# Routed layers of a decoder kernel: gated slot results scattered into pairs of rows, read back by plain loads, with 23 and 31 steps

## The chip, the cores and the metric

The kernel runs on one core of one Trainium2 chip. The metric is the device time of one execution in microseconds (us); lower is better. TensorE, VectorE (DVE in the rows), ScalarE (ACT), GpSimd (POOL) and SyncE (SP) each run their own list of instructions in order and wait for each other on semaphores. DMA transfers are issued from SP's and POOL's queues.

## The reference

A residual stream x of 4 x 512 tokens (T = 2048) and 512 features goes through four attention-like layers and four feed-forward layers. The change is in the last and the third feed-forward layer, which are routed:

```python
# ffn2: 8 experts, inner size 352, top 2, gates renormalised
topk_w, topk_i = jax.lax.top_k(softmax(x @ gate_w.T), 2)
topk_w = topk_w / jnp.sum(topk_w, axis=-1, keepdims=True)
for e in range(8):
    w_e = jnp.sum(jnp.where(topk_i == e, topk_w, 0.0), axis=-1)
    out = out + w_e[:, None] * ((silu(x @ w_gate[e]) * (x @ w_up[e])) @ w_down[e])
# ffn3: 16 routed experts, inner size 256, gelu, top 2, gates not renormalised,
# and two shared experts for all tokens
x = x + tanh(g_ffn[i]) * out          # x inside the layer is its layer norm
```

## The kernel before

Each token takes two experts, so there are 4096 pairs of token and choice. `router_block` computes the logits, takes the top two, counts the tokens per expert and gives each pair a slot; each expert's slots begin at a multiple of 256. A step is 256 slots of one expert. The number of steps, NS, is fixed: 2T/256 + experts = 24 in ffn2 and 32 in ffn3. By matmuls with one-hot matrices (hot_p, hot_h) the router inverts the map: `step_token` says for each slot which token it holds. `step_expert` holds each step's expert, `slot` each pair's slot, and `gates` its weight, times tanh of the layer's gate.

`routed_block` then runs the loop over steps. Two buffers, w = 0 and 1, alternate. In the order of their names in the code:

- SP: load(s+2) brings the expert's weights to mo_up (up32) and mo_dn (dn32), once step s's are split into halves; store(s-1) waits for the results of s-1 (o_done) and writes mo_o (o32) to `slot_results`.
- POOL: gather(s+1) waits until step s-1 was transposed (g_T), copies two columns of step_token (L810), and fetches 2 x 128 rows of the normalised x by indirect DMA (L814) into mo_g.
- TensorE: transposes of s+1 (L852), the up matmuls of s (L867), the down matmuls of s-1 (L882). TensorE's step s therefore starts with the transposes of s+1.
- ScalarE: y_high(s+1) (L904), per chunk the silu or gelu (L926, L928) and the high half of mid (L932), with the high halves of the next weights between (L911, L918); results(s-1) (L938) moves the down result from PSUM to mo_o.
- VectorE: the low half of each of these (L962, L967, L974, L984) and in ffn2 the product (L981).

All precise values are kept as a high and a low half in f16, with three matmuls in place of one.

After the loop comes the read-back: POOL waits for all stores, and gathers for each token tile of 128 the two result rows (L835), four indirect DMAs for two tiles. VectorE multiplies by the gates (L1011, L1016), adds to x (L1019) and computes bn_stats (L1023) for the next layer norm. At the end of the program `store_block` writes x with one DMA of 4 MB (L3357). Blocks follow one another; all engines meet between them. The names in rows leave out a block's number, so mo_ stands for both layers.

Of the kernel before, what the change touches and what calls it, by code (L numbers as in the profile page):

```python
# [16 lines left out]
P = 128  # L17
# [236 lines left out]
SLOTS = 256  # L254
ROUND = 12582912.0


def router_block(nc, env, y_hi, y_lo, w_router, n_exp, coef, routing, th, down_scale, renorm, shared):
# [7 lines left out]
    gates, slot, step_expert, step_token = routing  # L266
    NS = step_expert.shape[1]
    with ExitStack() as ctx:
# [13 lines left out]
        slotf, tile = sb("slotf", [P, NT, 2]), sb("tile", [P, NT, 2])  # L282
        stepi, stepf, owner = sb("stepi", [P, NS], I32), sb("stepf", [P, NS]), sb("owner", [P, NS])
# [3 lines left out]
        hot_h = sb("hot_h", [P, NT * 2, 2 * NS], F16)  # L287
        p_rank, p_total = ps("rank", [P, NT, n_exp]), ps("total", [P, NT, n_exp])
        p_token = ps("slot_token", [P, 2 * NS])
        tri_clear, tri_done, hot_ready, counted = sem("tri_clear"), sem("tri"), sem("one_hots"), sem("counted")  # L290
        placed, inverted = sem("places"), sem("inverted")
# [14 lines left out]
        def _(pool):  # L306
# [3 lines left out]
            nc.gpsimd.iota(ramp_p[:], pattern=[[1, P]], base=0, channel_multiplier=0).then_inc(ramp_done, 1)  # L310
            nc.gpsimd.memset(ones[:], 1.0).then_inc(tri_done, 1)
# [14 lines left out]
        def _(pe):  # L326
# [16 lines left out]
            for n in range(2 * NT):  # L343
                last = nc.tensor.matmul(p_token[:], hot_p[:, n, :], hot_h[:, n, :], start=(n == 0), stop=(n == 2 * NT - 1))
            last.then_inc(inverted, 1)

        @block.vector
        def _(dve):
# [4 lines left out]
            dve.wait_ge(ramp_done, 4)  # L353
# [26 lines left out]
            c.link(nc.vector.tensor_scalar(gates[:], tops[:], cs[:], None, ALU.mult))  # L380
# [5 lines left out]
            c.link(nc.vector.tensor_copy(stepf[:], stepi[:]))  # L386
            dve.wait_ge(counted, 2)
# [17 lines left out]
            c.link(nc.vector.tensor_copy(slot[:], slotf[:]))  # L405

            for i in (tokenf, token), (ramp_pf, ramp_p):
                c.link(nc.vector.tensor_copy(i[0][:], i[1][:]))
# [6 lines left out]
            def spread(v, n):  # L415
# [5 lines left out]
            h4 = hot_h[:].rearrange("p (t j) h -> p t (j h)", j=2)  # L421
            nc.vector.tensor_tensor(h4, h4, tokenf[:].unsqueeze(2).to_broadcast([P, NT, 4 * NS]), ALU.mult
                                    ).then_inc(placed, 1)
# [8 lines left out]
            c.link(nc.vector.tensor_copy(step_token[:], p_token[:]))  # L432
# [266 lines left out]
def routed_block(nc, env, rows, slots_out, w_up, w_down, kind, inner, routing):  # L699
# [4 lines left out]
    gates, slot, step_expert, step_token = routing  # L704
# [10 lines left out]
    CT = HS  # L715
    with ExitStack() as ctx:
# [11 lines left out]
        cur_slot = sb("cur_slot", [P, 2, CT, 2], I32)  # L728

        back = [t[:].rearrange("p w h d -> p (w h) d").rearrange("p (j u) d -> p j u d", j=2) for t in (g, o32)]  # L730
# [5 lines left out]
        g_in, back_in = ([env.dma_sem(f"{n}{i}") for i in range(2)] for n in ("rows_in", "results_in"))  # L736
# [4 lines left out]
        dn_done, o_done, stored, all_stored = sem("down_done"), sem("out_done"), [sem("out0"), sem("out1")], sem("stored")  # L741
        slot_done, added = sem("slot_cur"), sem("x_added")
        add_own, load_go = sem("add_dve"), sem("load_go")
        block = ctx.enter_context(nc.Block())

        def run_steps(engine, step):

            for s in range(2):
                step(s, s, s < 1, s < 2, False)
            with engine.Fori(1, NS // 2 - 1) as i:  # L750
                step(i * 2, 0, False, False, False)
                step(i * 2 + 1, 1, False, False, False)
            for s in (NS - 2, NS - 1):
                step(s, s % 2, False, False, s == NS - 1)
# [9 lines left out]
        def _(sp):  # L764
# [24 lines left out]
            def store(s, w):  # L789
                sp.wait_ge(o_done, HS * (s + 1))  # L790
                sp.sem_inc(load_go, 1)
                sp.dma_start(slots_out[bass.ds(s * SLOTS, SLOTS), :].rearrange("(h p) d -> p h d", p=P),
                             o32[:, w, :, :]).then_inc(stored[w], 16)
            for w in range(2):
                sp.sem_inc(stored[w], 16)
# [3 lines left out]
            store(NS - 1, 1)  # L799
            sp.wait_ge(stored[0], 16 * (NS // 2 + 1))  # L800
            sp.wait_ge(stored[1], 16 * (NS // 2 + 1))
            sp.sem_inc(all_stored, 1)

        @block.gpsimd
        def _(pool):
# [2631 lines left out]
```

## Time and profile before

| | |
|---|---|
| median of 3 runs | 3375.85 us (3372.21 to 3376.14) |
| the profiled execution | 3385.13 us, its span 3383.4 us |
| mean granted TensorE clock | 0.879 |
| busy over the span | TensorE 74%, VectorE 66%, ScalarE 47%, GpSimd 33% |
| ffn2: loop, read-back | 1851.5 to 2181.2, then to 2244.9 us |
| ffn3: loop, read-back, store | 3089.7 to 3306.7, to 3368.6, to 3383.4 us |

The profiled execution is a run of its own, so its time is not among the three. A duration in a row is that of one instruction or group; "idle before" with an arrow names what ended the wait. Records of DMA instructions on a queue are the issue alone; the landing is given apart. The other layers, from 0 to 1767 us and from 2246 to 2922 us, are the same in both kernels.

### The profile page before, as it was taken

The numbers are of one execution on the slowest core, as the hardware profiler recorded it, in microseconds if no ns is written. First come the engines' busy times: TensorE is split into PE (matmuls) and PEld (weight loads), VectorE is DVE, ScalarE is ACT, GpSimd is POOL, SyncE is SP. The second block draws the span as 40 slices with busy tenths as digits, with TensorE's granted clock in tenths as the row PEclk, the third lists the DMA queues.
The fourth block names the chain that finished last, engine by engine and source line by source line (L and its number), as shares of the span: only waits on it lengthen the run. The fifth ranks groups of instructions, "written<-read, shape, count | busy, mean of one in ns | idle before, by whom it ended". The sixth has DMA issues, their size and how long they took to land. (4 is left out here: it accounts for less than half of the span.)

```text
span 3383.4 us, 41979 instructions
## 1 busy us (share of the span) xinstructions
PE 2518.9 (74%) x14172; PEld 1210.4 (36%) x14172; DVE 2237.8 (66%) x3608; ACT 1606.1 (47%) x2265; POOL 1125.3 (33%) x814
## 2 busy tenths in 40 slices
PE   2987997799788727666653999719788888668990
PEld 1532333344343202222222777505322222334660
DVE  6665763444366788998986666565688884646664
ACT  2544554254334645545532555415476674224870
POOL 5755764010001126666651222155500000002434
PEclk9988999899889858899985999959799999778995
DMA  3640221110000000000003777536402201104995
GB/s 128 203 166 22 80 78 75 59 63 1 4 1 12 0 1 0 0 0 0 0 0 117 233 248 234 157 106 218 168 8 76 63 14 63 51 25 155 316 304 167
DMA packets 162836, 306.01 MB, mean 90 GB/s; under 512 B 33300, under 2 KB 80672, under 8 KB 160247
## 3 DMA queue, kind: packets, MB, share of 16 engines
q1 hardware_dynamic: 139462, 223.49, 19.1%
q0 software_dynamic: 23216, 80.49, 8.3%
q8 instruction: 90, 1.47, 0.2%
q14 instruction: 68, 0.55, 0.1%
HBM read 210.34 MB, written 93.32 MB: 90 GB/s over the span
## 5 line engine op out<-in xcount | busy, mean ns | idle before, releaser
L2054 DVE TENSOR_REDUCE ac_nmax<-ac_M 128x1 f32<-128x512 f32 (+1 forms) x768 | 497.2, 687 | 152.2 <-PE ac_M L1868 147.6
L2032 ACT ACTIVATE ac_PT<-ac_S 128x1024 f32<-128x1024 f32 x384 | 371.2, 1017 | 161.1 <-PE ac_S L1903 142.9
L3190 POOL TENSOR_TENSOR sc_hc<-sc_h,sc_cs 128x1024 f32<-128x1024 f32 x128 | 300.6, 2354 | 172.1 <-DVE sc_h L3304 119.6
L3304 DVE TENSOR_TENSOR_SCAN sc_h<-sc_dA,sc_dB 128x1024 f32<-128x1024 f32 x128 | 292.1, 2283 | 7.0 <-ACT sc_dA L3270 7.0
L3225 PE MATMUL sc_y<-sc_hc,ident 128*128 128x512 f32 x512 | 253.8, 626 | 2.6 <-POOL sc_hc L3190 2.6
L3270 ACT ACTIVATE sc_dA<-ss_delta,sc_A 128x511 f32<-128x511 f32 x256 | 166.0, 682 | 31.7 <-DVE sc_h L3304 31.4
L3203 PE MATMUL sc_b<-ss_bc,sc_sel 128*128 128x512 f16 x128 | 54.7, 428 | 162.0 <-DVE sc_dB L3296 128.7
L3296 DVE TENSOR_TENSOR sc_dB<-ss_du,sc_b 128x1024 f32<-128x1024 f32 x128 | 156.1, 1220 | 27.9 <-PE sc_b L3203 16.9
L3275 ACT ACTIVATE sc_cs<-sc_c 128x512 f32<-128x512 f32 x128 | 76.2, 596 | 202.6 <-POOL sc_hc L3190 159.5
L1868 PE MATMUL ac_M<-KT,QT 64*128 64x512 f16 (+1 forms) x384 | 141.6, 431 | 40.3 <-DVE ac_nmax L2054 23.2
L814 POOL DMA_INDIRECT mo_g<-normalised,mo_cur x112 | 145.3, 1297 | 61.3 <-POOL mo_cur L810 44.2
L967 DVE SCALAR_TENSOR_TENSOR mo_up16l<-mo_up,mo_up16h 128x1408 f16<-128x1408 f32 (+1 forms) x80 | 117.1, 1465 | 71.2 <-ACT mo_up16h L911 70.8
L810 POOL COPY mo_cur<-step_token 128x2 int32 (+1 forms) x56 | 15.4, 276 | 394.4 <-PE mo_yT L852 265.1
L867 PE MATMUL mo_pu<-mo_y16h,mo_up16h 128*128 128x256 f16 (+1 forms) x832 | 127.5, 276 | 25.7 <-DVE mo_up16l L967 11.0
L3225 PEld LDWEIGHTS sc_y<-sc_hc,ident 128*128 128x128 f32 x512 | 104.2, 204 | 99.1 <-issue 80.0
L1868 PE MATMUL ac_M<-ac_KT,ac_QT 64*128 64x512 f16 (+1 forms) x384 | 122.3, 386 | 23.2 <-DVE ac_nmax L2054 18.2
L1922 PE MATMUL ac_o<-ac_PT,ac_V 128*32 128x512 f32 x1024 | 137.9, 611 | 0.2
L1383 PE MATMUL ap_t<-ident,ap_y 128*128 128x128 f32 x128 | 20.4, 284 | 148.6 <-DVE ap_y L1569 148.6
L974 DVE SCALAR_TENSOR_TENSOR mo_dn16l<-mo_dn,mo_dn16h 128x1024 f16<-128x1024 f32 x80 | 83.0, 1062 | 71.5 <-ACT mo_dn16h L918 67.3
L867 PE MATMUL mo_pu<-mo_y16l,mo_up16h 128*128 128x256 f16 (+1 forms) x832 | 126.3, 275 | 0.0
L867 PE MATMUL mo_pu<-mo_y16h,mo_up16l 128*128 128x256 f16 (+1 forms) x832 | 126.0, 274 | 0.0
L932 ACT ACTIVATE mo_mid16h<-mo_mid 128x256 f16<-128x256 f32 x136 | 56.6, 417 | 132.3 <-DVE mo_mid L981 125.3
(515 smaller groups left out, 6102.3 us busy)
## 6 DMA issues: line engine op xcount, KB each, us to landing
slot_results<-mo_o SPq DMA_DIRECT2D x56, 512.0 KB, 3.9
mo_up<-in_w_gate SPq DMA_DIRECT2D x24, 704.0 KB, 5.5
mo_up<-in_w_up SPq DMA_DIRECT2D x24, 704.0 KB, 7.0
keys_t<-ap_kto SPq DMA_DIRECT2D x32, 512.0 KB, 2.6
queries_t<-ap_qto SPq DMA_DIRECT2D x32, 512.0 KB, 2.6
mo_up<-in_exp_up SPq DMA_DIRECT2D x32, 512.0 KB
mo_dn<-in_exp_down SPq DMA_DIRECT2D x32, 512.0 KB
mo_dn<-in_w_down SPq DMA_DIRECT2D x24, 512.0 KB
```

The costliest lines, as they stand in the source:

```text
L814: pool.indirect_dma_start(g[:, w, h, :], None, rows, bass.IndirectOffsetOnAxis(cur[:, w, h:h + 1], 0)).then_inc(g_in[w], 16)
L867: last = nc.tensor.matmul(pu[q][0:n, j, :], up16[h][:, w, j, k, c * P:c * P + n], y16[a][:, w, k, :], start=(i == 0), stop=(i == len(passe ...
L967: nc.vector.scalar_tensor_tensor(out=up16[1][:, w, j, :, :], in0=up32[:, w, j, :, :], scalar=SW, in1=up16[0][:, w, j, :, :], op0=ALU.mult, ...
L1868: nc.tensor.matmul(psM[:, slot, :], QT[b % 2][base:base + n, c, j * P:(j + 1) * P], KT[b % 2][base:base + n, :, c, :], start=True, stop=Tr ...
L1922: last = nc.tensor.matmul(po[r * VC:(r + 1) * VC, :], V[b % 2][:, kt, g % NG * GH + r, :], PT[:, m % PTB, i, :], start=(kt == 0), stop=(kt ...
L2032: nc.scalar.activation(PT[:, n % PTB, :, :], psS[:, 2 * (n % 2):2 * (n % 2) + 2, :], ACT.Exp, scale=SCALE / (SQK * SQK)).then_inc(exp_done, 1)
L2054: last = v.tensor_reduce(out[:, :, 0], sc[:, 0:MAIN], AX.X, ALU.max)
L3190: nc.gpsimd.tensor_tensor(hc[:, m % RC, :, :], h[:, m % RH, :, :], cs[:, m % 2, :].unsqueeze(1).to_broadcast([P, W, S]), ALU.mult).then_in ...
L3225: last = nc.tensor.matmul(py[:, c, :], env.id32[:], hc[:, m % RC, c, :], start=(n == 0), stop=(n == NS - 1))
L3270: last = nc.scalar.activation(dA[:, m % 2, c, 1:S], delta[:, b * KD + k, 1:S], ACT.Exp, scale=A[:, k, n:n + 1])
L3296: nc.vector.tensor_tensor(dB[:, m % RB, :, :], chans(du, b, p), pb[:].unsqueeze(1).to_broadcast([P, W, S]), ALU.mult).then_inc(dB_done, 1)
L3304: nc.vector.tensor_tensor_scan(h[:, m % RH, :, :].rearrange("p c s -> p (c s)"), dA[:, m % 2, :, :].rearrange("p c s -> p (c s)"), dB[:, m ...
```

## The change

1. The router also computes, for each slot, the row in a new tensor `result_pairs` (two rows per token, one per choice; slots without a token get a row of their own behind) and the slot's gate. For that it inverts two more one-hot products: the choice, and the gate in a high and a low half. `gates` and `slot` are gone.
2. ScalarE scales the results by the gate as it moves them to mo_o. It first copies the step's two gate columns.
3. POOL scatters mo_o by indirect DMA into `result_pairs` where SP stored it to `slot_results`. The gathers are issued one place earlier in POOL's order: gather(s+2), then the scatter of s-1.
4. The read-back is a plain SP load of 512 KB per token tile into four buffers of their own. VectorE adds the two rows, adds them to x, and computes bn_stats in ffn2 only. In ffn3 SP stores each tile of x as soon as it is done; `store_block` is gone.
5. NS is (2T + 255 x experts) / 256, rounded down: 23 and 31. The loop is unrolled for the first four steps.

```diff
@@ router_block
-            c.link(nc.vector.tensor_scalar(gates[:], tops[:], cs[:], None, ALU.mult))
+            c.link(nc.vector.tensor_copy(top_h[:], tops[:]))
+            c.link(nc.vector.tensor_tensor(rest[:], tops[:], top_h[:], ALU.subtract))
+            c.link(nc.vector.tensor_scalar(top_l[:], rest[:], GATE_LOW, None, ALU.mult))
+            c.link(nc.vector.tensor_copy(trashf[:], trash[:].rearrange("p s h -> p (s h)")))
...
-            c.link(nc.vector.tensor_copy(slot[:], slotf[:]))
...
+            for i, part in enumerate((top_h, top_l)):
+                last = nc.vector.tensor_tensor(hot_g[:, :, i, :], hot_h[:], spread(part[:], 2 * NS), ALU.mult)
+            last.then_inc(gates_placed, 1)
...
-            c.link(nc.vector.tensor_copy(step_token[:], p_token[:]))
+            c.link(nc.vector.tensor_scalar(step_token[:], p_token[:, 0, :], -1.0, 0.0, ALU.add, ALU.max))
+            c.link(nc.vector.scalar_tensor_tensor(out=pad[:], in0=p_token[:, 0, :], scalar=0.0, in1=trashf[:],
+                                                  op0=ALU.is_equal, op1=ALU.mult))
+            c.link(nc.vector.tensor_scalar(rowf[:], p_token[:, 0, :], 2.0, -2.0, ALU.mult, ALU.add))
+            c.link(nc.vector.tensor_tensor(rowf[:], rowf[:], p_token[:, 1, :], ALU.add))
+            c.link(nc.vector.tensor_tensor(step_row[:], rowf[:], pad[:], ALU.add))
+            dve.wait_ge(gates_inverted, 1)
+            c.link(nc.vector.tensor_scalar(pad[:], p_gate[:, 1, :], 1.0 / GATE_LOW, None, ALU.mult))
+            c.link(nc.vector.tensor_tensor(pad[:], pad[:], p_gate[:, 0, :], ALU.add))
+            c.link(nc.vector.tensor_scalar(step_gate[:], pad[:], cs[:], None, ALU.mult))
@@ routed_block, SP
-                if not first:
-                    store(s - 1, 1 - w)
...
+            for w in range(2):
+                sp.wait_ge(placed_rows[w], 16 * HS * ((NS + 1 - w) // 2))
+            def fetch(t):
+                sp.dma_start(back[:, t % NBK, :, :], pairs[2 * t * P:2 * (t + 1) * P, :].rearrange("(p j) d -> p j d", j=2)
+                             ).then_inc(back_in[t % NBK], 16)
+            for t in range(NBK):
+                fetch(t)
+            for t in range(NT):
+                sp.wait_ge(x_done, t + 1)
+                if t + NBK < NT:
+                    fetch(t + NBK)
+                if final:
+                    sp.dma_start(env.out[t * P:(t + 1) * P, :], env.x[:, t, :]).then_inc(x_out, 16)
@@ routed_block, POOL
+            def place_rows(s, w):
+                if not (isinstance(s, int) and s < 2):
+                    pool.wait_ge(placed_rows[w], 8 * HS * (turns(s, w) - 2))
+                    pool.sem_inc(g_go, 1)
+                nc.gpsimd.tensor_copy(cur_row[:, w, :], step_row[:, bass.ds(s * HS, HS)]).then_inc(row_done, 1)
+                pool.wait_ge(row_done, s + 1)
+                pool.sem_inc(g_go, 1)
+                pool.wait_ge(o_done, HS * (s + 1))
+                pool.sem_inc(g_go, 1)
+                for h in range(HS):
+                    pool.indirect_dma_start(pairs, bass.IndirectOffsetOnAxis(cur_row[:, w, h:h + 1], 0), o32[:, w, h, :], None).then_inc(placed_rows[w], 16)
+
             def step(s, w, first, early, last):
-                if not last:
-                    gather(s + 1, 1 - w, not first)
+                if not (isinstance(s, int) and s + 2 >= NS):
+                    gather(s + 2, w, True)
+                if not first:
+                    place_rows(s - 1, 1 - w)
@@ routed_block, ScalarE
+                nc.scalar.activation(cur_gate[:, w, :], step_gate[:, bass.ds(s * HS, HS)], ACT.Copy).then_inc(gate_done, 1)
+                act.wait_ge(gate_done, s + 1)
+                act.sem_inc(act_go, 1)
                 for h in range(HS):
                     act.wait_ge(dn_done, HS * s + h + 1)
-                    nc.scalar.activation(o32[:, w, h, :], po[h][:], ACT.Copy).then_inc(o_done, 1)
+                    nc.scalar.activation(o32[:, w, h, :], po[h][:], ACT.Copy, scale=cur_gate[:, w, h:h + 1]).then_inc(o_done, 1)
@@ routed_block, VectorE
+            for t in range(NT):
+                dve.wait_ge(back_in[t % NBK], 16 * (t // NBK + 1))
+                a, b = back[:, t % NBK, 0, :], back[:, t % NBK, 1, :]
+                nc.vector.tensor_tensor(a, a, b, ALU.add).then_inc(pair_done, 1)
+                dve.wait_ge(pair_done, t + 1)
+                nc.vector.tensor_tensor(env.x[:, t, :], env.x[:, t, :], a, ALU.add).then_inc(x_done, 1)
+                if not final:
+                    dve.wait_ge(x_done, t + 1)
+                    nc.vector.bn_stats(out=env.stats[:, t, :], in_=env.x[:, t, :])
@@ layer_ffn
-        NS = 2 * T // SLOTS + n_exp
+        NS = (2 * T + n_exp * (SLOTS - 1)) // SLOTS
```

In the rows of order below, the name in brackets is the semaphore waited for, under the name of its first use in the program. This is POOL's queue in the loop of ffn3, one step of it, before; row_in1_79 is g_T:

```order
L808 ISA
L810 ISA [waits row_in1_79]
L810 COPY mo_cur<-step_token 128x2
L811 ISA
L814 DMA mo_g<-normalised,mo_cur 128x512 [waits out_read_138]
L814 DMA mo_g<-normalised,mo_cur 128x512
```

And the same step now, where mid_hi_134 is g_T, q_roots_50 the landed scatters of the same buffer, and vd_out1_68 is o_done:

```order
L839 ISA [waits mid_hi_134]
L839 COPY mo_cur<-step_token 128x2
L840 ISA
L843 DMA mo_g<-normalised,mo_cur 128x512 [waits down_done_136]
L843 DMA mo_g<-normalised,mo_cur 128x512
L848 ISA
L850 ISA [waits q_roots_50]
L850 COPY mo_cur_row<-step_row 128x2
L851 ISA
L853 ISA [waits vd_out1_68]
L856 DMA result_pairs<-mo_o,mo_cur_row 12032x512 [waits first_batch_in_69]
L856 DMA result_pairs<-mo_o,mo_cur_row 12032x512
```

Behind each pair of gathers there now stand a copy, a wait for the step's results, and two scatters; the next gather comes after them.

On ScalarE, at the results in ffn3's loop, before (v_out1_66 is the down matmuls' semaphore, q_out0_63 the landed store):

```order
L935 ISA
L937 ISA [waits q_out0_63]
L938 ACTIVATE mo_o<-mo_po 128x512 [waits v_out1_66]
L937 ISA
L938 ACTIVATE mo_o<-mo_po 128x512 [waits v_out1_66]
```

and now (k_final_51 is the landed scatters, vd_out0_67 the end of the gate copy, ac_dve_70 the down matmuls):

```order
L962 ISA
L964 ISA [waits k_final_51]
L964 ACTIVATE mo_cur_gate<-step_gate 128x2
L965 REGISTER_ALU
L968 ISA [waits vd_out0_67]
L969 ACTIVATE mo_o<-mo_po,mo_cur_gate 128x512 [waits ac_dve_70]
L968 ISA
L969 ACTIVATE mo_o<-mo_po,mo_cur_gate 128x512 [waits ac_dve_70]
```

A copy of 128x2 and a wait for its own end stand ahead of the two activations.

At the end of the program on SP, before (v_out0_65 is o_done):

```order
L792 DMA slot_results<-mo_o 128x2x512 [waits v_out0_65] x3
L716 UNCONDITIONAL_BRANCH [waits q_out1_64,q_out0_63]
L3355 UNCONDITIONAL_BRANCH [waits barrier_Pool_Activation_PE_DVE_SP_release]
L3357 DMA out_x<-x_res 128x16x512
L3351 UNCONDITIONAL_BRANCH [waits k_T_57]
```

and now (k_out0_61 is x_done):

```order
L820 DMA mo_back<-result_pairs 128x1024 [waits k_final_51,q_roots_50]
L820 DMA mo_back<-result_pairs 128x1024 x3
L820 DMA mo_back<-result_pairs 128x1024 [waits k_out0_61]
L829 DMA out_x<-x_res 128x512
L820 DMA mo_back<-result_pairs 128x1024 [waits k_out0_61]
L829 DMA out_x<-x_res 128x512
```

SP issues the loads of the pairs itself, and a tile's store follows the addition to that tile.

## Rows read from the trace of the kernel before

**Rows 1.** Windows: start:end, length, busy us of each engine, clock, DMA share, GB/s.
```profile
1600.00:1700.00 100.00, 64.98 (x167) 25.56 (x166) 92.28 (x56) 54.45 (x85) 63.89 (x28) 0.95 0.00 0
...
1864.00:2168.00 304.00, 290.85 (x2237) 225.87 (x2236) 192.85 (x251) 180.83 (x297) 61.89 (x60) 1.00 0.72 229
...
2181.20:2244.90 63.70, 0.00 (x0) 0.00 (x0) 37.08 (x64) 0.00 (x0) 39.10 (x40) 0.53 0.49 140
...
3089.70:3306.70 217.00, 201.97 (x1408) 142.79 (x1408) 136.15 (x160) 169.88 (x288) 83.77 (x90) 0.98 0.90 297
```
**Rows 2.** The chain that ended last, ffn3's loop: start us, us, what.
```profile
3083.66 6.01 DMA mo_g<-normalised,mo_cur
...
3089.72 1.98 PE mo_yT L852 x8
...
3107.20 0.87 PE mo_yT L852 x8
...
3291.11 0.87 PE mo_yT L852 x8
...
3306.09 0.61 ACT mo_o L938
```
**Rows 3.** Timeline of ffn3's loop: start us, us, engine, what, idle before.
```profile
3113.12 1.04 PE L852 MATMUL mo_yT<-ident,mo_g 128*128 128x128 f32 x8
...
3119.20 1.04 PE L852 MATMUL mo_yT<-ident,mo_g 128*128 128x128 f32 x8
...
3119.40 0.60 ACT L938 ACTIVATE mo_o<-mo_po 128x512 f32<-128x512 f32 x1 [0.39 <-PE mo_po L882]
...
3120.25 0.40 SPq L792 DMA_DIRECT2D slot_results<-mo_o  x1
...
3120.51 0.18 POOL L810 COPY mo_cur<-step_token 128x2 int32 x1 [2.09 <-PE mo_yT L852]
...
3121.48 1.56 POOL L814 DMA_INDIRECT mo_g<-normalised,mo_cur  x1 [0.79 <-POOL mo_cur L810]
...
3123.35 1.16 POOL L814 DMA_INDIRECT mo_g<-normalised,mo_cur  x1 [0.31 <-issue]
```
**Rows 4.** ffn3's gathers: by group (busy, mean ns), by tile (ns least/median/most).
```profile
L814 POOL DMA_INDIRECT mo_g<-normalised,mo_cur x56 | 70.4, 1258 | 30.6 <-POOL mo_cur L810 22.0 <-issue 8.6
...
L814 POOL DMA_INDIRECT mo_g<-normalised,mo_cur x56: 960/1158/1968, 3102.6 to 3281.0; - x56
```
**Rows 5.** mo_g in ffn2's loop, from the start of the instruction.
```profile
DMA to landing us min/median/max: 4.3/4.4/5.4
```
**Rows 6.** Timeline of ffn2's loop.
```profile
2031.94 1.06 ACT L938 ACTIVATE mo_o<-mo_po 128x512 f32<-128x512 f32 x2
...
2037.32 0.64 PE L867 MATMUL mo_pu<-mo_y16h,mo_up16h 128*96 128x256 f16 x4 [0.54 <-DVE mo_mid L981]
...
2043.87 1.04 PE L852 MATMUL mo_yT<-ident,mo_g 128*128 128x128 f32 x8
...
2045.30 1.06 ACT L938 ACTIVATE mo_o<-mo_po 128x512 f32<-128x512 f32 x2
```
**Rows 7.** ScalarE's groups by form, the smallest activation.
```profile
L145 ACT ACTIVATE tanh_gates<-su_graw 128x8 f32<-128x8 f32 x1 | 0.2, 208 | 8.1 <-DMA su_graw<-in_g_ffn 8.1
```
**Rows 8.** Timeline of VectorE in ffn2's router.
```profile
1837.33 1.76 DVE L422 TENSOR_TENSOR rt_hot_h<-rt_hot_h,rt_tokenf 128x1536 f16<-128x1536 f16 x1
...
1841.81 0.21 DVE L432 CAST step_token<-rt_slot_token 128x48 int32<-128x48 f32 x1
```
**Rows 9.** Groups in ffn2's read-back.
```profile
L1023 DVE BATCH_NORM_STATS2 x_stats<-x_res x16 | 10.2, 681 | 0.0
...
L1019 DVE TENSOR_TENSOR x_res<-x_res,mo_g 128x512 f32 x8 | 5.1, 685 | 0.0
```
**Rows 10.** DMA issues: count, KB each, median us from issue to landing.
```profile
f_up<-in_up_weight_t SPq DMA_DIRECT2D x8, 512.0 KB, 4.3
...
out_x<-x_res SPq DMA_DIRECT2D x1, 4096.0 KB, 12.6
```

More of the change, by code:

```diff
@@ L343, in _ @@
             for n in range(2 * NT):
-                last = nc.tensor.matmul(p_token[:], hot_p[:, n, :], hot_h[:, n, :], start=(n == 0), stop=(n == 2 * NT - 1))
+                nc.tensor.matmul(p_token[:, 0, :], hot_p[:, n, :], hot_t[:, n, :], start=(n == 0), stop=(n == 2 * NT - 1))
+            for n in range(1, 2 * NT, 2):
+                last = nc.tensor.matmul(p_token[:, 1, :], hot_p[:, n, :], hot_h[:, n, :], start=(n == 1),
+                                        stop=(n == 2 * NT - 1))
             last.then_inc(inverted, 1)
+            pe.wait_ge(gates_placed, 1)
+            for n in range(2 * NT):
+                last = nc.tensor.matmul(p_gate[:], hot_p[:, n, :], hot_g[:, n, :, :], start=(n == 0),
+                                        stop=(n == 2 * NT - 1))
+            last.then_inc(gates_inverted, 1)
         @block.vector
@@ L404, in _ @@
                 c.link(nc.vector.tensor_reduce(slotf[:, :, j], h[:], AX.X, ALU.add))
-            c.link(nc.vector.tensor_copy(slot[:], slotf[:]))
-            for i in (tokenf, token), (ramp_pf, ramp_p):
-                c.link(nc.vector.tensor_copy(i[0][:], i[1][:]))
+            c.link(nc.vector.tensor_scalar(tokenf[:], token[:], 1.0, None, ALU.add))
+            c.link(nc.vector.tensor_copy(ramp_pf[:], ramp_p[:]))
             c.link(nc.vector.tensor_scalar(tile[:], slotf[:], 1.0 / P, -(P - 1) / 2 / P, ALU.mult, ALU.add))
@@ L696, in _, with routed_block @@
             expert(n_exp - 1, 1, False)
-def routed_block(nc, env, rows, slots_out, w_up, w_down, kind, inner, routing):
-    gates, slot, step_expert, step_token = routing
+def routed_block(nc, env, rows, pairs, w_up, w_down, kind, inner, routing, final):
+    step_expert, step_token, step_row, step_gate = routing
     NS = step_expert.shape[1]
@@ L727, in routed_block @@
         o32 = sb("o32", [P, 2, HS, D])
-        cur_slot = sb("cur_slot", [P, 2, CT, 2], I32)
-        back = [t[:].rearrange("p w h d -> p (w h) d").rearrange("p (j u) d -> p j u d", j=2) for t in (g, o32)]
+        cur_row, cur_gate = sb("cur_row", [P, 2, HS], I32), sb("cur_gate", [P, 2, HS])
+        back = sb("back", [P, NBK, 2, D])
         pT = ps("yT", [P, KD, SLOTS])
@@ L895, in _ @@
             run_steps(pe, step)
-            down(NS - 1, 1, False)
+            down(NS - 1, (NS - 1) % 2, False)
         @block.scalar
@@ L955, in _ @@
             run_steps(act, step)
-            results(NS - 1, 1)
+            results(NS - 1, (NS - 1) % 2)
         @block.vector
@@ L1001, in _ @@
             run_steps(dve, step)
-            with dve.Fori(0, NT // (2 * CT)) as i:
-                for v in range(2):
-                    dve.wait_ge(back_in[v], (i + 1) * (16 * 2 * CT))
-                    for n in range(3):
-                        for u in range(CT):
-                            t = (2 * i + v) * CT + u
-                            a, b = back[v][:, 0, u, :], back[v][:, 1, u, :]
-                            if n == 0:
-                                nc.vector.tensor_scalar(a, a, gates[:, bass.ds(t, 1), 0], None, ALU.mult
-                                                        ).then_inc(add_own, 1)
-                                continue
-                            dve.wait_ge(add_own, (2 * i + v) * (2 * CT) + (n - 1) * CT + u + 1)
-                            if n == 1:
-                                nc.vector.scalar_tensor_tensor(out=a, in0=b, scalar=gates[:, bass.ds(t, 1), 1], in1=a,
-                                                               op0=ALU.mult, op1=ALU.add).then_inc(add_own, 1)
-                            else:
-                                nc.vector.tensor_tensor(at(env.x, t), at(env.x, t), a, ALU.add).then_inc(added, 1)
-                    for u in range(CT):
-                        t = (2 * i + v) * CT + u
-                        dve.wait_ge(added, t + 1)
-                        nc.vector.bn_stats(out=at(env.stats, t), in_=at(env.x, t))
+            for t in range(NT):
[7 more added lines that the diff above has]
+                    nc.vector.bn_stats(out=env.stats[:, t, :], in_=env.x[:, t, :])
 def layer_ffn(nc, env, index):
@@ L3374, in build_program @@
             env.recycle()
-        store_block(nc, env, out)
 def laid_out(v):
```

100 lines of the change are left out of this document (39 added, 61 removed).

## The prediction

> **What bounds the kernel now.** I first split the two routed layers into stages by engine and clock [rows 1], then followed the chain of waits [rows 2] and the timeline of a few steps [rows 3, 6]. The layers are index 2 (ffn2, 24 steps before) and index 3 (ffn3, 32 steps). Each has three parts that follow one another: the router, the loop over steps, and the part that brings the results back and adds them to x.
>
> In ffn2's loop TensorE is busy for 291 of 304 us [rows 1], but it isn't what sets the pace. The same pair of result activations stands 13.36 us apart from one step to the next, and TensorE waits 0.54 us in between for VectorE's mo_mid [rows 6]. ScalarE and VectorE hand work to each other in a ring (results, weights high, weights low, mid, mid high) without slack, and TensorE follows that ring. In ffn3's loop a full step of TensorE takes 6.08 us, from one transpose to the next [rows 3]. 217.0 us for 32 steps is 6.8 on average; the DMA engines are 90% busy there at 297 GB/s [rows 1]. The read-back of ffn2 takes 63.7 us without any TensorE work [rows 1]. In ffn3 the read-back, the block for the store, and the store of 4096 KB (12.6 us [rows 10]) last from the last result, 3306.7 [rows 2], to the end of the span, 3383.4: 76.7 us.
>
> **The change, part by part.**
>
> *Router, two times.* Of the new vector work the two products into hot_g are large. The product of the same shape takes 1.76 us at 1536 columns [rows 8]. At 1472 columns two of them make 3.4 us, at 1984 columns 4.5 us. The tail behind the inversion grows from one small operation to eight, at 0.21 us and 0.03 between them [rows 8]: +1.7 us. Four small ones ahead of the counts replace two that go, and partly fill VectorE's wait for the counts: nothing (uncovered, 4 times 0.21 = 0.8 us). TensorE gets 16 matmuls for the row bit and 32 for the gates; VectorE's own work of 6 to 10 us lies over them; I add 0.4 us in ffn2, where the cover is thin. Sum: 5.5 + 6.2 = **+11.7**. If hot_g runs at half of that, 4 us less.
>
> *ffn2's loop.* One step less: -13.36. ScalarE copies the step's gates (128x2) ahead of the results, in the ring without slack. The smallest activation of the trace takes 0.21 us [rows 7]; with the wait for its own end I take 0.30 per step, 22 times: +6.6. (Bounds 0 and 0.6: 6.6 less or more. In the upper one is what the results' own activation may take longer now that its scale comes from a tile, which no row prices.) Pool now issues the results too. They end 2033.00, 0.3 later with the gate copy; 0.25 to hand over; two scatters, then the copy of indices and two gathers, by the sum below 10.0 us to landing: 2043.5, wanted at the next transpose, 2043.87 plus the 0.3 [rows 6]. It just fits. Net **-6.8**.
>
> *ffn3's loop.* This is the term that decides. Before, a gather follows the transpose that frees its buffer. Now Pool's order is: gather step s+2, wait for the results of s-1, scatter them, then gather s+3. The gather has to stand behind a wait for results which come at the end of TensorE's step, and its rows are wanted one step later. So from transpose k+2 to transpose k+4, two steps, the following must fit end to end:
>
> - TensorE's step 6.08, until the results' end 0.80 (3119.20 to 3120.00), hand-over 0.25 to a queue (3120.25) [rows 3]: 7.13
> - two scatters. None is in the trace; I price them as gathers, same rows and bytes, 1.26 mean [rows 4], 0.31 between [rows 3]: 2.83
> - index copy 0.18, 0.79 until the first gather, 0.31 between the gathers [rows 3], the first gather 1.26, landing 4.4 from the start of the second [rows 5]: 6.94
> - 0.2 for hand-overs in Pool's queue, an estimate from the 0.05 between landing and transpose in the chain, four times [rows 2].
>
> 17.1 us for two steps, 8.55 each, against 6.57 now (3107.20 to 3291.11, 28 steps [rows 2]). The cur_row copy costs nothing while Pool waits for results anyway; ScalarE's gate copy likewise lies in its wait for the down matmuls (uncovered, 30 times 0.3 = 9 us). Transpose 3 is still as before, 17.5 us after the first [rows 2]. Transpose 4 waits for place(0), which starts 1.05 after transpose 3: 17.5 + 1.05 + 2.83 + 6.94 + 0.2 = 28.5. Transpose 30 is 13 pairs later: 28.5 + 13 x 17.1 = 250.8. Behind the last transpose come 15.6 us as before (3291.11 to 3306.70 [rows 2]): 266.4 instead of 217.0, **+49.4**. Bounds: scatters and gathers at their least 0.96 [rows 4] and 4.3 to landing give 15.8 a pair and +31; all at the longest, 1.97, and 6.0 to landing as for the first gather [rows 2] give 20.8 and +102. I stay near the lower one, since the mean holds for this very stage.
>
> SP no longer has stores between its weight loads. That would help if weights were late; at 8.55 us per step they aren't.
>
> *Read-back of ffn2.* From the last result: 0.25, first scatter 1.0, 0.31, landing 4.4, then SP's plain load with 4.3 for 512 KB [rows 10]: 10.3 us to the first addition. Then VectorE per tile: two additions of 0.69 and bn_stats 0.68, each with 0.03 [rows 9]: 2.15 x 16 = 34.4. Sum 44.7 instead of 63.7: **-19.0**. Loads of 512 KB per 2.15 us are 244 GB/s, under the 297 that the DMA engines moved [rows 1]; four buffers are in flight. If the loads come singly at 297 and their 4.3 isn't covered, I lose 5.
>
> *Read-back and store of ffn3.* Loads start 6.0 after the last result; 8.39 MB in and 4.19 MB out, interleaved. VectorE needs only 1.45 per tile, so DMA sets it. At 297 GB/s [rows 1] 42.4 us: 48.4 instead of 76.7: **-28.3**. At the store's own 333 GB/s (4.19 MB in 12.6 us [rows 10]) -33; at 244 GB/s -19.
> The Trainium skill, DMA: Bandwidth & Descriptors, Specifications, gives some 358 GB/s as a core's share of HBM; by that the phase would last 35 us and the term be -35. The trace's 297 lies under it.
>
> Sum: 11.7 - 6.8 + 49.4 - 19.0 - 28.3 = **+7.0 us** on the profiled execution's 3385.13, which lies 9.3 above the median of the runs. Against that median, 3375.85: **3383 us**.
>
> **Rivals.**
> *The gather is in time* (0.15). The buffer is free two steps ahead as before, and if scatters are much cheaper than gathers, or ready results let Pool run ahead, ffn3 stays at its pace and even loses a step, 6.6 us. Then the term is -6.6 instead of +49.4: 3327 us. Against it: even at 0.96 each the pair takes 15.8, and it decides only under 13.1.
> *VectorE slows Pool's descriptors* (0.12). The gathers take 0.96 to 1.97 us [rows 4], the long ones beside vector work, and now there are twice as many. All four at 1.97 add 2.84 to each pair: +40 in ffn3. In ffn2 the rows then land at 2046.4, 2.2 us after they are wanted; TensorE's own 0.54 of waiting covers a part, the other 1.7 falls on each pair of steps: +18. 3441 us. Below a mean of 1.13 my sum has the other sign; above it this wait decides for slower.
> The Trainium skill, same page, SWDGE vs HWDGE vs iDMA, says that Pool writes its descriptor rings in SBUF while VectorE in its two-port mode locks it out, and that DMAs from SP are immune; this speaks against moving the results from SP to Pool. By that rule the long durations agree.
> *TensorE's clock* (0.06). It is granted 0.98 in ffn3's loop [rows 1], and now it would stand still for 4.9 us of each 17.1. At 1.2 instead of 2.4 GHz a step takes 6 us more; a fifth of the loop costs +17: 3400. Against: in the scan, 65% busy, it keeps 0.95 [rows 1].
> *The plain loads are slow* (0.05): 244 GB/s in both phases, +14: 3397.
>
> **How the numbers follow.** My forecast, 0.62, has its own range of 3362 to 3405: the terms' bounds partly cancel. 0.2% is 6.75 us, about what a measurement of this kernel tells from no change. Of the 0.62, 0.18 lies below 3369, 0.19 between, 0.25 above 3383. With the rivals: faster 0.33, same 0.19, slower 0.48. The range 3325 to 3425 leaves out half of the first rival, the upper part of the second and a little of the third: 0.16.
>
> **What would show it.** In the changed trace: transposes in ffn3 alternate, 17 us per two steps, waiting for the DMA of mo_g; Pool's scatter waits for ScalarE's mo_o and stands ahead of a late gather; ffn2's results 13.66 us apart; first addition 10 us after the last result; 2.15 us per tile in ffn2; the last store ends 48 us after the last result. I am wrong if TensorE never waits for mo_g in ffn3, or a scatter on Pool takes a quite different time than a gather.

## The result and the profile after

The changed kernel takes 3419.74 us (median, 3416.29 to 3425.3), the kernel before 3375.99 us on the same chip: a ratio of 1.0134, interval 1.0116 to 1.0151, so it is 43.75 us slower. I had forecast slower as the likeliest direction, by 7 us. 3419.74 lies outside the 3362 to 3405 that I gave the forecast itself, and inside 3325 to 3425, which was made wider for the rivals.

The profiled execution of the changed kernel took 3416.29 us, with a span of 3414.5. That is 31 us over the profiled one of before. The parts that the change doesn't touch were 12 us shorter in this one execution (9.1 ahead of ffn2's norm, 1.7 between the two layers, 1.2 in ffn3's shared experts and what stands between them and the loop), so the touched parts account for 43.2, which agrees with the medians.

Windows of the changed kernel, columns as in [rows 1]: ffn2's loop, the 13 pairs of steps in ffn3 whose transposes pause, ffn3 from the last result to the end, and ffn3's whole loop.
```profile
1847.00:2180.00 333.00, 303.99 (x2254) 232.00 (x2254) 196.53 (x253) 195.18 (x323) 116.60 (x131) 0.97 0.64 214
3096.00:3356.00 260.00, 191.48 (x1144) 134.52 (x1144) 112.63 (x130) 150.21 (x260) 122.07 (x157) 0.84 0.63 210
3373.10:3414.50 41.40, 0.00 (x0) 0.00 (x0) 21.87 (x32) 0.02 (x1) 2.59 (x4) 0.55 0.85 327
3068.00:3373.10 305.10, 227.24 (x1364) 159.71 (x1364) 134.17 (x155) 179.20 (x310) 138.12 (x177) 0.84 0.61 204
```
ffn3's loop took 217.0 us at a granted clock of 0.98 and 297 GB/s [rows 1]; now it takes 305.1 at 0.84 and 204 GB/s. TensorE does less work (31 steps for 32) and is busy 25 us longer: the same matmuls run at 1.2 GHz in part.

The chain of waits through one pair of steps in ffn3 (start us, us, what), to be held against [rows 2]:
```profile
3151.60 4.29 DMA mo_g<-normalised,mo_cur
...
3156.03 1.96 PE mo_yT L878 x8
3157.99 4.66 PE mo_pu L893 x24
3162.65 2.60 PE mo_po L908 x12
...
3165.28 0.70 ACT mo_o L969
...
3166.78 0.28 POOL result_pairs L856
...
3168.09 0.98 POOL result_pairs L856
3169.08 0.21 POOL mo_cur L839
...
3170.09 0.31 POOL mo_g L843
...
3172.01 4.25 DMA mo_g<-normalised,mo_cur
...
3176.38 1.97 PE mo_yT L878 x8
```
It is the chain of the forecast: transpose, up and down matmuls, the second result, two scatters, index copy, two gathers, landing, the transpose after the next. The transposes behind a pause take 1.97 us, where [rows 2] have 0.87. The timeline shows both kinds, and the pause:
```profile
3156.03 1.96 PE L878 MATMUL mo_yT<-ident,mo_g 128*128 128x128 f32 x8 [5.11 <-DMA mo_g<-normalised,mo_cur]
...
3157.78 1.06 PE L893 MATMUL mo_pu<-mo_y16h,mo_up16h 128*128 128x256 f16 x4
...
3165.07 1.04 PE L878 MATMUL mo_yT<-ident,mo_g 128*128 128x128 f32 x8
...
3165.28 0.69 ACT L969 ACTIVATE mo_o<-mo_po,mo_cur_gate 128x512 f32<-128x512 f32 x1 [0.60 <-PE mo_po L908]
...
3165.95 0.60 PE L893 MATMUL mo_pu<-mo_y16h,mo_up16h 128*128 128x256 f16 x4
...
3166.78 1.01 POOL L856 DMA_INDIRECT result_pairs<-mo_o,mo_cur_row  x1 [7.12 <-ACT mo_o L969]
```
Four up matmuls take 1.06 us behind the pause and 0.60 eight us later. The granted clock goes the same way. Around this pause, columns as in [rows 1]:
```profile
3155.30:3162.00 6.70, 5.97 (x28) 4.72 (x29) 1.58 (x2) 2.21 (x4) 3.13 (x5) 0.50 0.93 313
3162.00:3175.60 13.60, 9.32 (x62) 5.90 (x59) 7.09 (x9) 9.42 (x17) 6.09 (x8) 1.00 0.45 154
```
The first of these stretches begins as TensorE's pause of 5.11 us ends. 1.2 GHz is granted in it, 2.4 GHz in the second. From one paused transpose to the next the trace has 20.04 us on average (3096.21 to 3356.69, 13 pairs).

The waits of the same stretch, 3096 to 3356 (total us, times, longest):
```profile
POOL result_pairs L856 <- ACT mo_o L969: 84.7, 13, 7.4
...
PE mo_yT L878 <- DMA mo_g<-normalised,mo_cur: 66.1, 13, 5.5
```

In ffn2 TensorE now waits for gathers too, 16 times between 1864 and 2150, 20.4 us in all. Four rows of the timeline, and the landing of mo_g's gathers between 1900 and 2150, from the start of the instruction; it was 4.3/4.4/5.4 [rows 5].
```profile
2006.20 1.26 ACT L969 ACTIVATE mo_o<-mo_po,mo_cur_gate 128x512 f32<-128x512 f32 x2 [0.21 <-ACT mo_cur_gate L964]
...
2008.28 1.01 POOL L856 DMA_INDIRECT result_pairs<-mo_o,mo_cur_row  x1 [7.01 <-ACT mo_o L969]
...
2012.88 0.96 POOL L843 DMA_INDIRECT mo_g<-normalised,mo_cur  x1 [0.30 <-issue]
...
2020.81 1.09 PE L878 MATMUL mo_yT<-ident,mo_g 128*128 128x128 f32 x8 [1.99 <-DMA mo_g<-normalised,mo_cur]
...
DMA to landing us min/median/max: 5.3/6.7/7.8
```

### The profile page after: what moved, and what is told of

The parts are those of the page before. It is cut to its first block and busy times, and to the rows that moved or that the text cites. A ratio compares the mean times of both kernels' runs of the same rounds, so it can differ in the third digit from the quotient of the medians.

```text
span 3414.5 us, 41425 instructions
## 1 busy us (share of the span) xinstructions
PE 2532.3 (74%) x14126; PEld 1223.3 (36%) x14126; DVE 2219.3 (65%) x3566; ACT 1617.8 (47%) x2297; POOL 1157.2 (34%) x892
## 5 line engine op out<-in xcount | busy, mean ns | idle before, releaser
L856 POOL DMA_INDIRECT result_pairs<-mo_o,mo_cur_row x108 | 108.7, 1006 | 322.3 <-ACT mo_o L969 289.5
L878 PE MATMUL mo_yT<-ident,mo_g 128*128 128x128 f32 x432 | 73.5, 326 | 122.8 <-DMA mo_g<-normalised,mo_cur 120.3
L998 DVE SCALAR_TENSOR_TENSOR mo_up16l<-mo_up,mo_up16h 128x1408 f16<-128x1408 f32 (+1 forms) x77 | 112.6, 1464 | 45.3 <-ACT mo_up16h L937 45.3
L843 POOL DMA_INDIRECT mo_g<-normalised,mo_cur x108 | 116.3, 1077 | 61.8 <-POOL mo_cur L839 43.2
L993 DVE SCALAR_TENSOR_TENSOR mo_y16l<-mo_yT,mo_y16h 128x1024 f16<-128x1024 f32 x54 | 65.7, 1216 | 100.8 <-ACT mo_y16h L930 85.6
```

Source lines behind the costliest of these rows:

```text
L843: pool.indirect_dma_start(g[:, w, h, :], None, rows, bass.IndirectOffsetOnAxis(cur[:, w, h:h + 1], 0)).then_inc(g_in[w], 16)
L856: pool.indirect_dma_start(pairs, bass.IndirectOffsetOnAxis(cur_row[:, w, h:h + 1], 0), o32[:, w, h, :], None).then_inc(placed_rows[w], 16)
```

## The experiments

Eight kernels ran. Times are medians; a ratio stands against the kernel before, on the same chip. Unless said otherwise the numbers of a period or a loop are starts of transposes in the profiled execution of that kernel.

**The gather ahead of the wait.** The only edit is the order in Pool's queue, in both layers. It needs no third buffer: transpose s+1, which frees the buffer of gather s+3, runs before the results of s-1 exist.
```
-                if not (isinstance(s, int) and s + 2 >= NS):
-                    gather(s + 2, w, True)
+                if not (isinstance(s, int) and s + 3 >= NS):
+                    gather(s + 3, 1 - w, True)
                 if not first:
                     place_rows(s - 1, 1 - w)
             gather(0, 0, False)
             gather(1, 1, False)
+            gather(2, 0, True)
```


> The gather of step s+3 is issued on Pool ahead of the wait for the results of step s-1, in both routed layers; nothing else changes. My theory (the order in Pool's queue is what costs ffn3 its 85 us): TensorE no longer stands still 5 us per two steps and keeps 2.4 GHz. What Pool does itself per step then sets the pace: 20.4 us per pair of steps now, less its wait of 7.1, is 6.65 per step, so the loop of ffn3 takes 215 to 225 us instead of 302.5. ffn2's loop loses its waits for mo_g, about 6 us. Total 3419.7 - 80 - 6 = 3334 us, under the kernel before. Rival (the scatters are dear by themselves: Pool's descriptors, or traffic into DRAM): they are all still there, so the total stays at 3400 or above.

Measured: 3345.91 us, ratio 0.9914 (0.9897 to 0.9932), so 74 us under the changed kernel and below the one before. ffn3's loop, first transpose to last result, takes 236.2 us instead of 305.1, at a clock of 0.95. In ffn2 no transpose after the second waits for a gather; they stand 14.01 us apart, where the changed kernel had 14.26 (1936.05 to 2149.96, 15 steps), and the loop falls from 331.9 to 328.3. The order is the cause of most of what ffn3's loop had lost, 68.9 of 88.2 us. The forecast of 215 to 225 for ffn3 was too low: 7.62 us per step (3090.85 to 3281.41, 25 steps), not 6.65. Pool now has no idle piece above 1.1 us there (3085 to 3265): its own instructions and the 0.30 to 1.0 between them fill the step.

**The gate read directly.** As before, and:
```
-                nc.scalar.activation(cur_gate[:, w, :], step_gate[:, bass.ds(s * HS, HS)], ACT.Copy).then_inc(gate_done, 1)
-                act.wait_ge(gate_done, s + 1)
...
-                    ... ACT.Copy, scale=cur_gate[:, w, h:h + 1])
+                    ... ACT.Copy, scale=step_gate[:, bass.ds(s * HS + h, 1)])
```


> As the gather ahead of the results' wait, and the results' activation reads its scale straight from the tile of all steps' gates, so that ScalarE's copy of two gates and its wait go. Theory (ScalarE and VectorE hand work round in a ring without slack in ffn2): 0.40 us less in each of 22 steps of ffn2, -9 us beside the kernel with the new order alone, and nothing in ffn3, where Pool sets the pace: 3325 us. Rival (the ring has slack, or something else paces ffn2 now): within 2 us of that kernel.

Measured: 3335.22 us, ratio 0.9877 (0.9861 to 0.9894). ffn2's period falls from 14.01 to 13.69 us, so copy and wait cost 0.32 per step, and ffn2's loop falls from 328.3 to 321.5; ffn3's period stays at 7.62.

**The scale a constant.** As the last, with `scale=0.5`; the gates are left out of the output.

> The kernel with the gather ahead and without the gate copy, and the results' activation scales by the constant 0.5 in place of the gate of each slot (the gates are left out of the output). Theory: a scale from a tile makes each of the two activations some 0.1 us longer (0.69 against 0.60), and in ffn2's ring both count in full: the period of ffn2's steps falls from 13.69 back to 13.36 us and 22 of them give -7 us. ffn3 unchanged. Rival (what is left of the difference to before comes from the gathers or scatters beside the ring): the period stays at 13.6 to 13.7.

Measured: 3323.88 us, in a single execution, so only the period is read from it. ffn2's is 13.42 us. The two activations with a scale from a tile cost the ring 0.27 us per step, and 0.06 over the 13.36 of before is not explained. Rows of the timeline of the three kernels, two transposes each, 14.01, 13.71 and 13.41 apart (neighbouring steps differ by 0.03); first the gather ahead,
```profile
2034.76 1.04 PE L879 MATMUL mo_yT<-ident,mo_g 128*128 128x128 f32 x8
...
2048.77 1.04 PE L879 MATMUL mo_yT<-ident,mo_g 128*128 128x128 f32 x8
```
then the direct gate,
```profile
2032.90 1.04 PE L879 MATMUL mo_yT<-ident,mo_g 128*128 128x128 f32 x8
...
2046.61 1.04 PE L879 MATMUL mo_yT<-ident,mo_g 128*128 128x128 f32 x8
```
and the constant.
```profile
2038.38 1.04 PE L879 MATMUL mo_yT<-ident,mo_g 128*128 128x128 f32 x8
...
2051.79 1.04 PE L879 MATMUL mo_yT<-ident,mo_g 128*128 128x128 f32 x8
```
None of the six has an idle time in brackets: the ring sets this pace, not the gathers.

**The pause filled.** The changed kernel, order kept; in ffn3 16 matmuls on a tile of zeros stand ahead of every second transpose.
```
                 if not last:
+                    if not gated and w == 1:
+                        for _ in range(16):
+                            nc.tensor.matmul(p_idle[:], env.id16[:], idle[:], start=True, stop=True)
                     transposes(s + 1, 1 - w, True)
```


> The changed kernel with its order kept, and 16 matmuls of 512 columns on a tile of zeros (3.4 us at 2.4 GHz) put into TensorE's pause ahead of every second transpose of ffn3. Their results go nowhere. Theory (TensorE restarts at 1.2 GHz after each pause, and pays 3.06 us from transpose to second result: 9.94 against 6.88): the granted clock of the loop rises from 0.84 to 0.95 or more, the pair of steps shrinks from 20.0 to 17.0 us, 13.5 pairs give -40: 3380 us. Rival (the slow step comes from something else than the clock, or the clock falls anyway): 3420 us or more.

Measured: 3392.79 us, ratio 1.0053 (1.0035 to 1.007), 27 us under the changed kernel by adding work. The window from 3096 to 3331,
```profile
3096.00:3331.00 235.00, 211.63 (x1358) 136.04 (x1357) 114.69 (x130) 152.65 (x260) 123.44 (x159) 0.99 0.69 234
```
and the timeline around one filled pause:
```profile
3196.25 1.09 PE L881 MATMUL mo_yT<-ident,mo_g 128*128 128x128 f32 x8 [0.87 <-DMA mo_g<-normalised,mo_cur]
...
3202.39 3.62 PE L921 MATMUL mo_fill_out<-mo_fill_in,ident 128*128 128x512 f16 x16
3206.26 0.98 PE L881 MATMUL mo_yT<-ident,mo_g 128*128 128x128 f32 x7 [0.25 <-DMA mo_g<-normalised,mo_cur]
```
The clock is 0.99 instead of 0.84; from 3150 to 3311 TensorE has no idle piece above 1.64 us. Two steps take 17.3 us (3154.81 to 3310.54, nine pairs), not 20.0; the first two and the last pair kept 19.5 to 20.4, so the loop fell by 25 us, to 279.9, and not by 40.

**A third scatter.** The changed kernel, and one more scatter of 128 rows per step in ffn3, into a tensor that nothing reads (waits on the scatters' semaphore count three per step there).
```
                 for h in range(HS):
                     pool.indirect_dma_start(pairs, ..., o32[:, w, h, :], None).then_inc(placed_rows[w], 16)
+                if final:
+                    pool.indirect_dma_start(spare, ..., fixed[:], None).then_inc(placed_rows[w], 16)
```


> The changed kernel with its order, and in ffn3 one more scatter of 128 rows per step, from a tile of zeros into a DRAM tensor that nothing reads. Theory (one chain: results, scatters, index copy, gathers, landing, transpose, two steps of TensorE per turn): each pair of steps grows by one scatter, 1.0 + 0.3, from 20.0 to 21.3 us; 14 turns give +18: 3438 us. Rival A (each of the two extra scatters of a pair counts, Pool being the bound): +36. Rival B (the scatters lie beside other work): within 5 us of 3420.

Measured: 3434.37 us, ratio 1.0156 (1.0139 to 1.0173). The pair of steps grew by 0.66 us to 20.70 (3099.75 to 3368.87, 13 pairs), the loop by 9.0: half of what I expected. Cut up link by link (means over 13 pairs), the link from the first scatter to the first gather grew by 1.32, as the theory says. But the second gather followed the first by 1.44 instead of 1.87, and the second result followed the transpose by 8.94 instead of 9.37; the landing took 0.20 more. The chain holds, and two of its links got shorter as it moved against the other engines. I didn't test why.

**Both index copies together.** The gather ahead, the direct gate, and in Pool's queue (`copy_rows` is the part of `place_rows` up to and with the copy of cur_row):
```
                 nc.gpsimd.tensor_copy(cur[:, w, :], step_token[:, bass.ds(s * HS, HS)]).then_inc(cur_done, 1)
+                if placing:
+                    copy_rows(s - 4, w)
+                    pool.wait_ge(row_done, s - 3)
...
-                    place_rows(s - 1, 1 - w)
+                    place_rows(s - 1, 1 - w, more)
```


> The kernel with the gather ahead and the direct gate, and on Pool the two copies of indices (cur and cur_row) of a step stand together ahead of the gathers, with one stall behind them; between the second gather and the first scatter only the wait for the results is left. Theory: in ffn3 Pool now sets the pace (7.4 us per step: four DMAs of some 1.15, 0.30 twice, a copy of 0.2 with 0.82 behind it, and a copy of 0.2 with 0.99 behind it). If a wait that is already met costs Pool nothing, the second copy with its 0.99 shrinks to 0.3 and 0.9 us per step goes, down to TensorE's own 6.1 to 6.6: -20 us in ffn3, 3315 us. If Pool pays 0.8 for every wait ahead of a DMA, met or not, only 0.4 per step goes: -10 us, 3325. Rival (the loop is paced by DMA traffic, 84% busy, and not by Pool's own instructions): 3335, no change.

Measured: 3334.43 us, ratio 0.9862 (0.9845 to 0.9878), which can't be told from the direct gate alone. The period of ffn3 fell from 7.62 to 7.36 us (3085.44 to 3269.45, 25 steps), the loop from 234.4 to 228.0. Pool's timeline:
```profile
3172.97 1.04 POOL L847 DMA_INDIRECT mo_g<-normalised,mo_cur  x1 [0.98 <-issue]
3174.32 0.97 POOL L847 DMA_INDIRECT mo_g<-normalised,mo_cur  x1 [0.31 <-issue]
3175.67 1.01 POOL L864 DMA_INDIRECT result_pairs<-mo_o,mo_cur_row  x1 [0.38 <-issue]
3176.98 0.98 POOL L864 DMA_INDIRECT result_pairs<-mo_o,mo_cur_row  x1 [0.30 <-issue]
3177.97 0.19 POOL L839 COPY mo_cur<-step_token 128x2 int32 x1
3178.10 0.18 POOL L854 COPY mo_cur_row<-step_row 128x2 int32 x1
3179.27 1.08 POOL L847 DMA_INDIRECT mo_g<-normalised,mo_cur  x1 [0.99 <-issue]
3180.65 1.41 POOL L847 DMA_INDIRECT mo_g<-normalised,mo_cur  x1 [0.30 <-issue]
3182.84 1.01 POOL L864 DMA_INDIRECT result_pairs<-mo_o,mo_cur_row  x1 [0.78 <-issue]
```
Between 3085 and 3265 Pool has three idle pieces above 1.1 us, of 1.5, 1.5 and 2.1, and a wait that is already met costs 0.30 to 0.38 between a gather and a scatter; one that is just being met costs 0.78, as in the last row. So 0.6 to 0.7 of the 0.99 went, but the step gained only 0.26. The wait behind the copies is now 0.99 where the one ahead of the gathers was 0.82, and Pool's idle time per step fell by 0.38 in all (2.50 to 2.11). The two copies got longer, 0.36 each for 0.27, and the four DMA instructions a little shorter, with a mean of 1.13 for 1.16, where the shortest take 0.96.

**Half of the weights.** As the last, with half of each load in ffn3 from its third step on; the other half stays stale in the buffer.
```
+                kt, ct = (KD // 2, full // 2) if reuse and not gated else (KD, full)
-                    sp.dma_start(up32[:, w, j, :, :], w_up[j][bass.ds(e, 1), :, :]...
+                    sp.dma_start(up32[:, w, j, 0:kt, :], w_up[j][bass.ds(e, 1), 0:kt * P, :]...
```


> The kernel with the gather ahead, the direct gate and the two index copies together (3334.4 us), and from the third step of ffn3 on only half of each expert's weights is loaded: the other half stays as it was in the buffer, so the output is that of mixed weights. TensorE, ScalarE, VectorE and Pool do the same work; a step moves 1.6 MB instead of 2.1. It asks what now holds ffn3's step at 7.31 us, between TensorE's 6.08 and the 6.57 of the kernel before. Theory (DMA traffic: 0.90 busy at 290 GB/s): the period falls to 6.6 or less, 28 steps give -20 us: 3314. Rival (Pool's own row of four DMAs, waits and copies): the period stays within 0.15 of 7.31 and the total within 5 us of 3334.

Measured: 3333.47 us, ratio 0.9876 (0.9859 to 0.9892), and a period of 7.33 us (3081.22 to 3264.59, 25 steps). The window of that loop:
```profile
3079.00:3270.00 191.00, 165.19 (x1153) 115.39 (x1151) 114.67 (x134) 149.53 (x238) 137.35 (x156) 0.99 0.68 214
```
and the same window of the kernel with full loads:
```profile
3079.00:3270.00 191.00, 169.42 (x1152) 118.35 (x1151) 112.52 (x131) 146.65 (x236) 133.85 (x155) 0.96 0.90 290
```
The DMA share fell from 0.90 to 0.68 and the step didn't move. DMA traffic isn't what holds the improved kernel. That Pool's row of instructions is, the rival, is read from the trace: between 3085 and 3265 Pool has one idle piece above 1.1 us. In the same change its DMA instructions went from a mean of 1.13 to 1.20 us, so less traffic didn't make them shorter.

**24 and 32 steps.** The gather ahead and the direct gate, with `NS = 2 * T // SLOTS + n_exp` and the loop's bounds moved to match.

> The kernel with the gather ahead and the direct gate, with 24 and 32 steps in place of 23 and 31. Theory: one more step costs its layer's period, 13.7 us in ffn2 (ring of ScalarE and VectorE) and 7.4 in ffn3 (Pool), with about 0.3 for the wider one-hots: +21 us, 3356. Rival (the last step is mostly hidden beside the rest of the drain): under +12.

Measured: 3361.49 us, ratio 0.9941 (0.9924 to 0.9957). Against the ratio without the step, 0.9877, that is 0.0064 or 22 us for one step in each layer, as expected. ffn2's loop is 13.4 us longer (334.9 against 321.5), ffn3's 9.9, where its period would give 7.6.

## Why the prediction was right in its mechanism and short by 37 us

The wait that was to decide, a late gather behind the results in Pool's queue, is there in every pair of steps. The direction rests on less: +7.0 us was the rest of terms between +49 and -28. By part, measured less forecast, the routers are off by -0.7, ffn2's loop by +9.0, ffn3's by +38.8, and the read-backs by -3.8 and -7.0.

*Routers, +11.7: right.* From the start of the norm to the first transpose ffn2 takes 5.0 us more; the tail of small operations ends 5.2 later. ffn3's router is 6.0 longer, up to the first instruction of the shared experts. VectorE in ffn2's router, against [rows 8]:
```profile
1830.17 1.69 DVE L441 TENSOR_TENSOR rt_hot_g<-rt_hot_h,rt_top_h 128x1472 f16<-128x1472 f16 x1
1831.77 1.68 DVE L441 TENSOR_TENSOR rt_hot_g<-rt_hot_h,rt_top_l 128x1472 f16<-128x1472 f16 x1
```
*ffn2's loop, -6.8: it is +2.2.* One step less is worth its 13.4 us (24 and 32 steps). The gate copy was taken at 0.30 and costs 0.32. The tile's scale, left out of the value and put in the upper bound, costs 0.27. And "it just fits" failed: the rows were to land 4.4 us after the second gather began; now the median is 6.7 (5.3 to 7.8), and the transposes come 0.25 us per step late. In the changed kernel the gathers start at 2011.59 and 2012.88, between SP's four weight loads from 2011.23 to 2013.62. Before, the gathers of a step began some 4 us ahead of the loads (2019.43 against 2023.35). Their new place beside these loads is a likely reason for the longer landing, the two scatters just ahead of them another; no run separates them. With the gather ahead the landing is as long (median 6.8) and nothing waits for it.

*ffn3's loop, +49.4: it is +88.2, which is the miss.* The way to transpose 4 was right (28.2 for 28.5), and the tail nearly so (16.4 for 15.6). The whole error lies in the pair of steps, 20.04 instead of 17.1, 13 times. Link by link, as means over the 13 pairs:

| link | forecast | measured |
|---|---|---|
| transpose to end of second result | 6.88 | 9.37 |
| hand-over to Pool | 0.25 | 0.82 |
| first scatter to first gather | 3.80 | 3.51 |
| first gather to second | 1.57 | 1.87 |
| second gather to transpose | 4.40 | 4.47 |
| allowance for hand-overs | 0.20 | - |
| pair | 17.10 | 20.04 |

The step that failed is the first: "TensorE's step 6.08", taken from a loop in which TensorE had no pauses and a clock of 0.98. I had the clock as a rival with 0.06, argued away with the scan, which keeps 0.95 at 65% busy. That mean hid the answer. The scan's idle time lies in pieces of 1.1 to 1.8 us, and there the clock is 1.00; the one longer pause between 1600 and 1700, of 5.2 us until 1644.29, is where the one stretch at 1.2 GHz begins, 1642.0 to 1652.2. In the trace of before, TensorE's row and the window:
```profile
1644.29 1.97 PE L3216 MATMUL sc_y<-ident,sc_yt 128*128 128x128 f32 x8 [5.20 <-POOL sc_yt L3181]
...
1642.00:1652.00 10.00, 5.93 (x15) 3.32 (x16) 8.67 (x7) 1.79 (x3) 4.54 (x2) 0.50 0.00 0
```
The pauses of the changed kernel are 4.8 to 5.5 us. The filled pause shows the price: with the clock at 0.99 the same link is 7.01 and the pair 17.3, all but 0.2 of the forecast. The clock costs 2.36 us of 2.94. The Trainium skill, TensorE: Matmul & The Clock Gate, Part 1, says that the clock is halved by default and that recent activity releases it, and that matmuls behind each other cost their columns over 1.2 or 2.4 GHz. As an estimate from that, a group of four with 256 columns is followed by the next after 0.85 us or 0.43; the trace has 0.85 (3157.78 to 3158.63) and 0.43 (3165.95 to 3166.38), so it agrees.

The hand-over was taken from the row of SP's queue, 0.25; Pool takes 0.82, every time. Scatters were priced as gathers, at 1.26; they take 0.98 to 1.01, which gives half of that back.

Three figures of the prediction don't follow from its own chain. It holds three DMA durations, not four, as the landing is counted from the second gather's start. All at 0.96 then give 16.1 a pair and not 15.8; all at 1.97 add 2.13 and not 2.84; and the mean at which the sum turns its sign is 1.09, not 1.13. None of it touches the 17.1.

*Read-backs, -19.0 and -28.3: -22.8 and -35.3.* The last scatter lands 2.7 after its start, not 4.4, and SP's first load in 3.1 (ffn2) and 3.5 (ffn3), not 4.3; a tile takes 2.05 for 2.15:
```profile
2181.24 0.97 POOL L856 DMA_INDIRECT result_pairs<-mo_o,mo_cur_row  x1 [0.30 <-issue]
2183.99 15.29 SPq L820 DMA_DIRECT2D mo_back<-result_pairs  x10
2187.14 0.69 DVE L1036 TENSOR_TENSOR mo_back<-mo_back 128x512 f32<-128x512 f32 x1 [14.70 <-DMA mo_back<-result_pairs]
```
In ffn3 the loads start 5.5 after the last result, where I had 6.0, and the rest is the rate, for which I took 297 GB/s:
```profile
3385.00:3409.00 24.00, 0.00 (x0) 0.00 (x0) 17.49 (x26) 0.00 (x0) 0.00 (x0) 0.50 1.03 398
```
297 had been moved beside other work and 333 by a single store; neither was a limit, and nor was the 358 of the prediction's sentence on the Trainium skill. From the first load to the last landing, 3378.66 to 3413.15, the mean is 365.

*The rivals.* The gather in time: no, TensorE waits in every pair, until the order is turned; then it is 3346 and not the 3327 that I priced, since Pool becomes the next limit. VectorE against Pool's descriptors: in the changed kernel 13 of 104 DMA instructions in ffn3 (3096 to 3356) take over 1.2 us, all of them beside vector work, and the mean is 1.07, under the 1.13 at which this was to decide; it didn't. Vector work beside them isn't enough for that: in ffn2, between 1900 and 2150, 67 of 69 have it and none takes over 1.01. The clock: yes, on top of the forecast and not instead of it, and larger than its +17: 13 pairs at 2.36 make 31. Of the sum, the routers' 11, ffn2's +2, ffn3's +88 and the read-backs' -58 make +43.

*What stays open:* why the first gather of a pair takes 1.61 us in 12 of 13 pairs of the changed kernel. All 13 long DMA instructions there lie beside VectorE's mo_mid16l and mo_up16l (L1015, L998), and none of the 91 others lies beside both. With the pause filled the first gather takes 0.99 to 1.25 and the second up to 1.98, and 9 of the 10 long ones (3150 to 3311) lie beside the same two. No run tested whether these two are the cause. Open as well is why Pool's DMA instructions are longer in ffn3 the more closely they follow each other: traffic isn't the reason, since with half of the weights the mean is 1.20, but VectorE is denser too (busy for 0.43 of the window in the changed kernel, for 0.59 and 0.60 in the last two).

## What to carry to other kernels

In an in-order queue, an instruction that only waits for something early (a freed buffer) belongs ahead of one that waits for something late (results), above all where rows are wanted a step later; here turning two lines was worth 74 us and turned a kernel 1.3% slower than before into one 0.9% faster, or 1.2% with the direct gate. Before a pause is priced, ask what the paused engine costs when it starts again: here TensorE's pauses of 5 us added another 2.4 each. A mean clock over a stage can hide a pause of that length; look at what came behind each one. And when work moves to another queue, take the hand-over from that queue's own rows.

## What the runs showed of the hardware that I had not expected

- Matmuls on zeros in a pause made the kernel 27 us faster, by holding the clock at 0.99 where it had been 0.84.
- Pool's DMA starts 0.82 us after the result that it waited for; behind a wait that is already met, 0.30 to 0.38. SP takes 0.25 [rows 3].
- An activation of 128x512 with its scale from a tile takes 0.68 us on average in ffn2, with a constant 0.58.
- A scatter of 128 rows of 2 KB to DRAM costs Pool the same 0.98 to 1.01 us as a gather where nothing lengthens it. It lands 2.7 us after its start at the end of a loop, with a median of 3.4 us in ffn3's loop, and of 6.5 there with the gather ahead.
